# Attention's hyperbolic units placed on a cycle of the batch, with the first value sums staged

## The reference

```python
tq = jnp.sqrt(1.0 / curv + jnp.sum(q * q, axis=-1, keepdims=True))
tk = jnp.sqrt(1.0 / curv + jnp.sum(k * k, axis=-1, keepdims=True))
inner = jnp.einsum('bhtd,bhsd->bhts', q, k) - tq * jnp.swapaxes(tk, -1, -2)
arg = jnp.maximum(-curv * inner, 1.0 + 1e-07)
dis = jnp.sqrt(1.0 / curv) * jnp.arccosh(arg)
scores = 1.0 / (eps + dis) + causal_bias
out = jnp.einsum('bhts,bhsd->bhtd', softmax(scores), v)
```

## Time and profile before

| what | value |
|---|---|
| median of three runs | 2300.5 us (2297.19 to 2304.39) |
| profiled execution, time | 2313.5 us |
| its span, first to last instruction | 2312.0 us |
| PE, ACT, DVE, POOL busy over the span | 78%, 62%, 62%, 30% |
| a middle batch of attention, slot 0 to slot 0 | 183.9 us |
| first batch, slot 0 to slot 0 | 200.9 us |
| from the last exponential of attention to the experts | about 67 us |

### The profile page before, as it was taken

One profiled execution on the slowest core, in us unless ns is written; L12 is line 12 of the kernel. 1 busy time (PEld: TensorE's weight loads), 2 busy tenths in 40 slices (PEclk: granted clock), 3 DMA queues, 4 the chain that ended last, 5 costly groups with the idle time before them and its releaser, 6 DMA issues. The chain is left out here.

```text
span 2312.0 us, 39981 instructions
## 1 busy us (share of the span) xinstructions
PE 1806.9 (78%) x13330; PEld 965.2 (42%) x13330; DVE 1422.5 (62%) x3280; ACT 1422.3 (62%) x1400; POOL 683.8 (30%) x332
## 2 busy tenths in 40 slices
PE   6888888843887896897797787888789689746994
PEld 3434443421333443343344343444434334325893
DVE  4767676772663776676676777776777667650113
ACT  1333333321887888788788888788788878811110
POOL 0000000001443534444444444543444365510002
PEclk9999999975997998998998999999899899878997
DMA  5222333328026006207306304504502620119972
GB/s 190 85 103 109 110 110 110 110 107 166 1 45 96 11 16 125 66 1 122 83 2 113 92 2 84 121 2 70 126 11 31 137 55 23 42 51 350 345 276 66
DMA packets 88461, 217.50 MB, mean 94 GB/s; under 512 B 14112, under 2 KB 34848, under 8 KB 83936
## 3 DMA queue, kind: packets, MB, share of 16 engines
q1 hardware_dynamic: 79840, 184.74, 30.5%
q0 software_dynamic: 8448, 30.41, 4.2%
HBM read 146.52 MB, written 68.58 MB: 93 GB/s over the span
## 5 line engine op out<-in xcount | busy, mean ns | idle before, releaser
L1067 ACT ACTIVATE a_PT<-a_s 128x1024 f32<-128x1024 f32 (+3 forms) x576 | 461.3, 808 | 206.8 <-PE a_s L889 135.0
L886 PE MATMUL a_s<-a_Q,a_K 96*128 96x512 bf16 (+7 forms) x1152 | 331.3, 350 | 157.0 <-ACT a_PT L1067 108.7
L1245 DVE TENSOR_REDUCE a_mx<-a_w 128x1 f32<-128x512 f32 (+2 forms) x576 | 305.9, 550 | 53.0 <-PE a_w L917 36.8
L1145 POOL TENSOR_TENSOR a_Z<-a_Z,a_R 128x2182 f32<-128x2182 f32 x64 | 290.4, 4537 | 94.0 <-ACT a_R L1079 94.0
L1142 POOL TENSOR_TENSOR a_R<-a_Z 128x2182 f32<-128x2182 f32 x64 | 244.6, 3822 | 217.2 <-DVE a_Z L1237 130.7
L245 PE MATMUL p_ps<-p_xT,p_w 128*128 128x512 f32 x512 | 248.0, 645 | 46.4 <-ACT p_xT L341 25.5
L901 PE MATMUL a_o<-a_PT,a_V 128*32 128x512 f32 (+3 forms) x2304 | 276.0, 554 | 6.4 <-ACT a_PT L1067 6.4
L1237 DVE TENSOR_SCALAR_CACHE_REDUCE a_Z<-a_w 128x512 f32<-128x512 f32 (+7 forms) x384 | 202.0, 530 | 120.2 <-PE a_w L929 85.3
L946 PE MATMUL a_w<-a_ident,a_R 128*128 128x128 f32 (+1 forms) x1152 | 207.4, 306 | 75.2 <-DVE a_PTh L1294 63.9
L1294 DVE COPY a_PTh<-a_w 128x512 f32<-128x512 f32 (+1 forms) x256 | 156.4, 618 | 141.0 <-PE a_w L946 138.8
L886 PEld LDWEIGHTS a_s<-a_Q,a_K 99*128 99x128 bf16 (+1 forms) x1152 | 111.0, 102 | 250.5 <-ACT a_PT L1067 140.6
(11 more groups left out here) (161 smaller groups left out, 2961.9 us busy)
## 6 DMA issues: line engine op xcount, KB each, us to landing
e_w<-in_w SPq DMA_DIRECT2D x23, 2048.0 KB, 8.5
qk_parts<-p_parts SPq DMA_DIRECT2D x32, 768.0 KB, 3.5
a_Q<-qk_parts SPq DMA_DIRECT2D x144, 128.0 KB, 4.7
a_K<-qk_parts SPq DMA_DIRECT2D x144, 128.0 KB, 6.6
v_rows<-p_vt SPq DMA_DIRECT2D x8, 2048.0 KB, 7.7
a_V<-v_rows SPq DMA_DIRECT2D x32, 512.0 KB, 8.1
p_xin<-in_x SPq DMA_DIRECT2D x8, 1024.0 KB, 6.7
a_X<-in_x POOLq DMA_DIRECT2D x8, 1024.0 KB, 11.3
```

What stands on the lines that cost most here:

```text
L886: m = pe.matmul(sB[x % 2][:, i, 0:w], Kb[0:r, h, P * j:P * j + P], Qb[0:r, h, t0:t0 + w], start=True, stop=not diag)
L1067: act.activation(PT[:, u % 2, 2 * k:2 * k + 2, 0:w], sB[x % 2][:, :, 0:w], ACT.Exp, scale=scale_of(GROUPS[g][2 * k])).then_inc(prob.sem, 1)
L1145: pool.tensor_tensor(z, z, r, ALU.add).then_inc(z_sum.sem, 1)
L1245: dve.tensor_reduce(mx[:, pc, col:col + 1], wB[x % WB][:, 0:w], AX.X, ALU.max).then_inc(wide_free.sem, 1)
```

## The change

- `LEAD, SPAN` are 12 and 122 instead of 6 and 113: the units' `ready` slots go from 6, 22, 38, 54, 70, 86, 102, 119 to 12, 29, 46, 64, 81, 99, 116, 134. The step to the next batch's unit 0 is 22 slots instead of 31. The last passes of unit 7 (`log_sum`, `log_distance`, `inverse`), its row bias and all its exponentials, and unit 6's turns now lie past slot 144, in the next batch: 28 wrapped items instead of 14. Unit 0's arguments stand in slots 4 to 10 instead of 0 to 5.
- The rounds of maxima start at steps 2 and 9 instead of 1 and 8; the second is done in 12 steps instead of 13.
- `turn_sums` 2, 5, 6, 7, 3, 4 move, 3 and 4 to slots 34 and 37 of the next batch (from 17 and 21). `O`'s first half of group 0 would be written at slot 19, ahead of them: so `copy_sums` 0 writes a new tile `early` of 128x512, and a new POOL item `unstage` at slot 41 copies that to `O`. PE's first `turn_sums` of a batch waits for it (`o_moved`).

```diff
--- before.py
+++ after.py
@@ -632,7 +632,7 @@
             work[u][VALUES if u < NQ else 0].append(("values", u - 1))
             if (u - 1) % 12 in (3, 11):
                 work[u][VALUES + 1 if u < NQ else 0].append(("sums", 2 * ((u - 1) // 12) + ((u - 1) % 12 == 11)))
-        LEAD, LAST = 6, 113
+        LEAD, SPAN = 12, 122
         wrapped = set()
 
         def put(at, item):
@@ -643,9 +643,9 @@
             work[at // NSLOT][at % NSLOT].append(item)
 
         for n in range(NU):
-            ready = LEAD + LAST * n // (NU - 1)
+            ready = LEAD + SPAN * n // (NU - 1)
             args = [("argument", n, k, pc) for k, seg in enumerate(segments(n)) for pc in range(len(seg[3]))]
-            span = 2 * len(args) if n else LEAD
+            span = 2 * len(args) if n else 8
             for a, item in enumerate(args):
                 put(ready - span + a * span // len(args), item)
             put(ready, ("square", n))
@@ -666,7 +666,7 @@
                 for part in range(2):
                     put(ready + 37 + part, ("hyp_values", HYP_TILES[n - 1 + part]))
 
-        ROUNDS = (((4, 5), 1, 1, 7), ((0, 1, 2, 3), 2, 8, 13))
+        ROUNDS = (((4, 5), 1, 2, 7), ((0, 1, 2, 3), 2, 9, 12))
         MAXIMA = [[(h, i, pc, s0, w) for h in hs for i in range(NT) for pc, (s0, w) in enumerate(pieces(i))]
                   for hs, _, _, _ in ROUNDS]
         for r, (_, _, first_step, steps) in enumerate(ROUNDS):
@@ -686,9 +686,10 @@
             work[11 + 2 * n][1].append(("project", n))
             work[12 + 2 * n][2].append(("statistics", 0, n, n + 1))
 
-        SUMS = {0: 117, 1: 121, 2: 125, 5: 147, 6: 151, 7: 155, 3: 161, 4: 165}
+        SUMS = {0: 117, 1: 121, 2: 143, 5: 148, 6: 152, 7: 156, 3: 178, 4: 181}
         for n, at in SUMS.items():
             put(at, ("turn_sums", n))
+        put(41, ("unstage",))
         work[2][0].append(("shift",))
         work[27][0].append(("variance", 0))
         work[27][3].append(("inverse_root", 0))
@@ -770,6 +771,7 @@
         nb = sb("a_nb", [P, 2, 4])
         PTh = sb("a_PTh", [P, NT + 1, 4, P])
         O = sb("a_O", [P, 4, T])
+        early = sb("a_early", [P, HB])
         X = sb("a_X", [P, NT, C])
         Y = sb("a_Y", [P, NT, H, HD])
         rden = sb("a_rden", [P, 2, H])
@@ -796,7 +798,7 @@
         score = ev("a_score", NQ * 2, carried=True)
         prob = ev("a_prob", NQ * 2, carried=True)
         valued = ev("a_valued", NQ, carried=True)
-        o_copied = ev("a_o_copied", 6, carried=True)
+        o_copied, o_moved = ev("a_o_copied", 6, carried=True), ev("a_o_moved", carried=True)
         wide_full, wide_free = ev("a_wide_full", n_wide, carried=True), ev("a_wide_free", n_wide, carried=True)
         m_step = ev("a_m_step", 12)
         z_sq = ev("a_z_sq", NU)
@@ -963,6 +965,8 @@
                 bank = wide_bank(b, index["turn_sums", n])
 
                 pe.wait_ge(o_copied.sem, o_copied.at(d, 4 if n < NT // 2 else 5))
+                if n == 0:
+                    pe.wait_ge(o_moved.sem, o_moved.at(d))
                 pe.wait_ge(wide_free.sem, wide_free.at(*ring(b, d, ("hyp_values", n), index)))
                 for g in range(4):
                     m = pe.transpose(bank[:, g * P:(g + 1) * P], O[:, g, n * P:(n + 1) * P], ident[:])
@@ -1150,6 +1154,11 @@
                     pool.wait_ge(h_prob.sem, h_prob.at(d, 4 * n + 2 * part + 1))
                     edge = R[:, n % RB, at:at + 2 * w].rearrange("p (f s) -> p f s", f=2)[:, :, w - GK:w]
                     pool.tensor_tensor(edge, edge, hmasks[:, 1], ALU.mult).then_inc(h_masked.sem, 1)
+                elif kind == "unstage":
+
+                    pool.wait_ge(o_copied.sem, o_copied.at(d, 0))
+                    hold(pool, wide_full.sem, wide_full.at(b, wide["turn_sums", NT // 2 - 1]), pool_passed)
+                    pool.tensor_copy(O[:, 0, 0:HB], early[:]).then_inc(o_moved.sem, 1)
                 elif kind == "shift":
                     pool.wait_ge(x_here.sem, x_here.at(d))
                     pool.tensor_tensor(X[:], X[:], bias[:].unsqueeze(1).to_broadcast([P, NT, C]), ALU.add) \
@@ -1187,6 +1196,7 @@
                     if is_last and u % 4 == 3 and u // 4 < NT:
                         spread_rows(u // 4)
 
+            o_moved.start(pool)
             rows_in(0)
             turn(0, is_first=True)
             with nc.Fori(1, B - 1, engines=[pool.engine], hint_back_edge=True) as b:
@@ -1306,7 +1316,12 @@
             def copy_sums(b, m):
                 g, c = divmod(m, 2)
                 dve.wait_ge(valued.sem, valued.at(b, 12 * g + (3 if c == 0 else 11)))
-                dve.tensor_copy(O[:, g, HB * c:HB * c + HB], oB[:]).then_inc(o_copied.sem, 1)
+                if m == 0:
+
+                    dve.wait_ge(o_moved.sem, o_moved.before(b))
+                    dve.tensor_copy(early[:], oB[:]).then_inc(o_copied.sem, 1)
+                else:
+                    dve.tensor_copy(O[:, g, HB * c:HB * c + HB], oB[:]).then_inc(o_copied.sem, 1)
 
             def divide_sums(b, d, n, x):
                 sums = wB[x % WB][:].rearrange("p (h w) -> p h w", w=VW)
```

## The result

The changed kernel takes 2358.3 us (median of four, 2349.4 to 2362.6) against 2300.5: ratio 1.0246, 95% interval 1.0212 to 1.0279. The forecast was 2292, with a range up to 2322. The profiled execution spans 2361.0 us, 49.0 more than before. In order of time: the first exponential of attention comes 2.5 us earlier, the first batch is 2.9 longer, the next six 34.0 together, the last 7.3, and all that follows the last exponential 7.3.

The account below looks back on a forecast made before the run. PE and ACT were taken to bound 24-slot stretches by turns, each its larger busy time plus old slack. Seven batches gave -10.5 us, the first -8, the tail +9.5: -9 in all, 2292 us, range 2262 to 2322.

Parts of the forecast that it names:

- 28.8+3.0: Slots 24 to 48 of a batch: PE's new busy time of 28.8 us plus 3.0 us of old slack.
- The wrap: Batch start: unit 0's square queues behind row load and shift on POOL; slot 24 at +31.8 us, not 29.3.
- pure balance: Slots 0 to 24 from busy time and old slack alone, without the late square: 23.0+2.9 = 25.9 us.
- DVE's stalls: DVE operations held beside POOL's: 3.19 us at slot 118, 1.0 of L1251's, 0.7 of the last stretch go.
- L1251's 1.0 us: Slots 72 to 96: the join of maxima, held 3.77 us before, gives back 1.0 us a batch.
- The carried slack: Every stretch but the first: its old slack, near 3 us, is added unchanged to the new larger busy time.
- The staging: Early sums copied back by POOL, later turns of sums: copy 0.9 us, hidden in POOL's idle, no cost.
- First batch and tail: Ends of attention: first batch 8 us shorter to slot 24; last mask behind rows and shift, 9.5 us longer.
- B: Chance 0.23: bad ACT and PE pairing within slots 24 to 48, slot 48 at 66.7, not 63.6; 2313 us.
- E: Chance 0.10: row bias (L1275, later L1285) held near the next unit's square, 2.3 us a batch; 2308 us.
- C: Chance 0.15: no change, as 1.5 us of the stall at the first normalization stay; 2302 us.
- D: Chance 0.15: rows land in 6.5 us or masks run early, slot 24 at +26.6, -5.2 a batch; 2256 us.

Follow-up runs that it names:

- rounds_back: The changed kernel with the maxima's rounds at their old steps (1 and 8, second in 13 steps): 2319.1 us, 1.004 of the kernel before.
- bias_reduce: The changed kernel with the row bias's two-input maximum done as a one-tensor reduction and its negation split in two: 2362.4 us, 1.0246 of the kernel before.
- shift_late: The changed kernel with the shift of the loaded rows at slot 22 instead of 8: 2325.6 us, 1.0096 of the kernel before.
- both: The changed kernel with the maxima's rounds as before and the shift at slot 22: 2295.5 us, 0.9968 of the kernel before.
- before_holds: The kernel before with normalizations at slots 115 and 131 instead of 113 and 129, second join at 83 instead of 85: 2334.7 us, 1.0131.
- join_alone: The kernel before with only the second round's join of maxima moved, slot 83 instead of 85: 2290.7 us, 0.9957.
- both_bias: The kernel of both, with log_distance, inverse and row_bias 14, 15 and 16 slots behind the square instead of 15, 17 and 19: 2378.3 us, 1.0331.

## Why the prediction was wrong

**The step that failed** is the sentence on the turn of the first round's maxima: "The turn maxima of round 0 come 4 slots later and still 9 slots ahead of their use, near 11 us, for a chain of two short loads; nothing." I asked who waits for its result, and not what its DVE operations meet on the way. At slot 39 the cast meets addition 1 and is held 4.45 us. This is most of the 5.4 us in the term "28.8+3.0" for slots 24 to 48; rounds_back takes 4.7 of them off and brings 39 us back.

**Behind it stands a wrong reading of the earlier trace rows.** I took the hold for one of operations with two inputs in SBUF, and searched the new order for those alone. The cast and bias_reduce's negation have one. The Trainium skill had both halves of the rule: "GPSIMD Engine Reference", section "Specifications", counts a two-port mode of VectorE too, and "VectorE: DVE Perf Modes", section "What auto-detection actually checks", gives such a mode to an instruction for which it is enabled when it has a single source, source and destination are in SBUF, and their outermost dimensions are both even or equal. I used the first half. The runs agree: cast (4.45 us) and negation (up to 2.3) are held, and the clamp, a tensor_scalar out of PSUM, is not (0.68 us inside an operation of POOL's as outside). The reduction has one source in SBUF too and isn't held (0.15 us); that section doesn't say for which instructions the mode is enabled.

**The wrap** was right: 5.03 us at slot 16 (4 to 6 forecast), slot 24 at 30.7 (31.8). Its size on the kernel, 33 us, is near the 5.9 us a batch that the term had over pure balance (41 for seven batches; the wait stands in six, 35). With the shift late, slots 0 to 24 take 24.4 us in shift_late and 25.5 in both; balance alone had given 25.9.

**The stalls removed** were right as far as they went, 3.3 us in slots 108 to 120 of before_holds (3.19), but "DVE's stalls" counted what goes and not what comes: 78 us held became 79. L1251's 1.0 us was right for the hold alone (1.1 at full clock in join_alone); with the low clock it is 2.1.

**The carried slack** was too small by 1.2 to 1.8 us in three stretches, 48 to 72 and those from 96 on, 4.4 a batch. The clock is no lower there than before (1.00, 0.84 and 0.95 against 0.95, 0.80 and 0.93). One part shows: ACT waits 13.9 us for the row bias in five batches, where it waited 5.3, so 1.7 a batch more, if all of it is on the path. The rest stays open.

**The granted clock** is nowhere in the sum, though a column of the earlier trace rows shows it. It fell where the new waits stand: 0.83 for 1.00 in slots 0 to 24, 0.86 for 0.89 in 24 to 48, and made the wait at slot 16 dearer, by 1.2 us (6.2 for 5.0). For the cast's wait the two aren't told apart: rounds_back takes off 4.7 us, and most of the low clock with it.

**The staging** at "nothing" was wrong on the old order (39 us, by the clock) and no run takes it out of the new one, where ACT bounds the stretch that it hurt.

**First batch and tail**: slot 24 of the first batch came 4.8 us earlier, not 8. Slots 12 to 24 of it take 15.4 us, and 10.7 in shift_late, though no shift stands in a first batch. This is the clock: it is 0.52 in the first and 1.00 in the second, and in rounds_back, with the shift where the change has it, 1.00 and 10.9 us. So some 4.5 us of the miss in the first batch are the low clock of this one execution. The tail grew by 7.3 (9.5 forecast).

**The rivals.** B's figure for slot 48, 66.7, is close to the 67.7 measured, and its reason is wrong: slot 36 came at +47.9, under its bound of +50, and the time is lost between 36 and 48. E happened, at a chance of 0.10: L1285 takes over 1 us 23 times in 64, and the held ones 44 us over the span. Its price is open: both has the same 47 us of holds, 31.1 us of waits of ACT behind them (7.5 before), and is still faster than before. C and D didn't happen. The forecast of 2292 is near the kernel with the two placements put back (2295.5), but that is luck: its batch is 180.2 and not 182.4, with another split over the stretches.

## What to carry to other kernels

When instructions are moved in a hand-written order, list for each one what runs beside it on the engine that can hold it, and not only who waits for its result: here a short SBUF to SBUF operation of VectorE behind a long one of GpSimd lasted until the long one ended, and everything queued behind it waited too. What counts is the order in time, which the order of the list doesn't fix (both_bias). Read the granted clock's column in each window before calling an engine's idle free; here 0.66 us of transposes taken out of an idle made the stretch 2.7 us longer. And when a hold is moved away, follow the chain behind it (here a store that lands 10.9 us after its issue) before the gain is counted.

## What the runs showed of the hardware that I had not expected

- A cast of 16x128 from SBUF to SBUF took 4.45 us instead of 0.21, and a tensor_scalar on two values up to 2.3 us instead of 0.17, while GpSimd's 128x2182 operation ran; a tensor_reduce of four values in SBUF, 0.15 us at the same place, was not held in 31 of 31 cases.
- 24 matmuls of zero weights, 1.5 us of useless work a batch (12.1 over eight), made a kernel of 2343 us 36 us faster: TensorE's clock stayed at its upper level (0.79 to 1.00 in that stretch). The Trainium skill's "TensorE: Matmul & The Clock Gate", Part 1, says that the gate follows how busy the engine was recently; the rows agree.
- A PE wait of 4.95 us made its stretch 6.2 us longer: the same 92 matmuls took 13.10 us instead of 11.05, at a clock of 0.81 instead of 1.00.
- A 128x2048 store issued behind the head loads landed after 9.9 to 10.9 us; issued ahead of them, after 5.9 to 6.0.
